# A deformable patch tokenizer rebuilt: convolution by slabs of the contraction, sampling points in squares of 8 rows by 4 columns, places spread by matmuls

## The reference, cut to what matters

```python
off = conv(x, offset_w, stride 16) + offset_b     # 2*256 offsets for each of 5 x 5 patches
py = 16*ho + ki + dy;  px = 16*wo + kj + dx       # 256 points of a patch, each moved by (dy, dx)
y0, x0 = floor(py), floor(px)
sampled = gather(y0, x0)*wy0*wx0 + gather(y0, x0+1)*wy0*wx1 \
        + gather(y0+1, x0)*wy1*wx0 + gather(y0+1, x0+1)*wy1*wx1
out = einsum('bhwkc,ock->bohw', sampled, dconv_w)
yn = batch_norm(out) * gamma + beta;  tokens = gelu(yn)
```

## Time and profile before

| | |
|---|---|
| median of 3 runs | 1245.86 us (1242.81 to 1247.65) |
| span of the profiled execution | 1245.7 us |
| PE busy | 913.0 us, 73% of the span |
| DVE busy | 587.2 us, 47% |
| ACT, POOL busy | 385.2 us, 301.6 us |
| mean granted TensorE clock | 0.829 |

### The profile page before, as it was taken

The page is one execution under the profiler, slowest core; times in us unless marked ns, Lnnn a source line. Parts: engine busy times, 40 slices in busy tenths (PEclk is TensorE's granted clock), DMA queues, the critical chain, the costliest instruction groups (busy, mean ns, idle before and its releaser), DMA issues. The chain is left out here.

```text
span 1245.7 us, 25546 instructions
## 1 busy us (share of the span) xinstructions
PE 913.0 (73%) x10115; PEld 768.6 (62%) x10115; DVE 587.2 (47%) x1245; ACT 385.2 (31%) x675; POOL 301.6 (24%) x291
## 2 busy tenths in 40 slices
PE   4937777769962993589985578487859999286584
PEld 1427777448852993478874566364549999265572
DVE  1639999445434323565442346554461111464463
ACT  0149888022220220244333223243201121143131
POOL 2048888023103231331110010100122322200100
PEclk9969999867875997699887589786777999697695
DMA  3559887570007552000000600000516992100000
GB/s 118 155 153 224 208 209 188 171 204 15 2 14 243 130 124 60 1 2 2 1 2 1 170 3 3 1 3 2 140 38 161 253 241 39 29 3 1 2 4 20
DMA packets 66359, 103.98 MB, mean 83 GB/s; under 512 B 15980, under 2 KB 50128, under 8 KB 66256
## 3 DMA queue, kind: packets, MB, share of 16 engines
q1 hardware_dynamic: 57776, 94.36, 29.5%
q0 software_dynamic: 5120, 4.88, 2.0%
q10 hardware_dynamic: 3360, 3.28, 0.7%
HBM read 92.45 MB, written 10.58 MB: 83 GB/s over the span
## 5 line engine op out<-in xcount | busy, mean ns | idle before, releaser
L1736 PE MATMUL ps_rows<-stage_strip,stage_hat_y 128*128 128x144 f32 x800 | 109.0, 293 | 40.0 <-DVE stage_product L1767 24.2
L1736 PEld LDWEIGHTS ps_rows<-stage_strip,stage_hat_y 128*128 128x128 f32 x800 | 101.6, 192 | 47.3 <-ACT stage_hat_y L1695 21.2
L1767 DVE TENSOR_TENSOR stage_product<-ps_rows,stage_hat_x 128x1296 f32<-128x1296 f32 x80 | 68.5, 898 | 14.1 <-PE ps_rows L1736 14.1
L1718 POOL TENSOR_SCALAR stage_hat_x<-stage_hat_x 128x480 f32<-128x480 f32 x41 | 74.3, 1813 | 3.2 <-ACT stage_hat_x L1693 3.0
L1775 DVE TENSOR_REDUCE stage_samples<-stage_product 128x1440 f32 x40 | 66.2, 1655 | 9.3 <-DVE stage_product L1767 9.3
L2543 DVE TENSOR_TENSOR L_ffnhid<-L_ffnact_gate,L_ffnbank_u 128x300 f32<-128x300 f32 x32 | 14.9, 467 | 117.6 <-ACT L_ffnact_gate L2561 117.6
L1690 ACT ACTIVATE stage_hat_y<-stage_hat_y,stage_w_minus_row 80x1280 f32<-80x1280 f32 x40 | 54.5, 1362 | 29.4 <-DMA stage_hat_y<-places_y 28.8
L1524 PE MATMUL ps_conv<-stage_w_offset_w,stage_patches 128*100 128x512 f32 x96 | 45.5, 628 | 17.2 <-DMA stage_patches<-in_patchesT 17.2
L1708 POOL TENSOR_TENSOR stage_hat_x<-stage_pos_xT,stage_w_window_x 128x240 f32<-128x240 f32 x80 | 48.4, 626 | 18.2 <-DVE stage_product L1767 16.5
L1695 ACT ACTIVATE stage_hat_y<-stage_hat_y 80x1280 f32<-80x1280 f32 x40 | 50.2, 1254 | 0.0
L1097 PE MATMUL L_attnbank_q<-L_attnhT,L_attnwq 128*128 128x200 f32 x192 | 42.7, 369 | 6.9 <-DVE L_attnqT L1262 6.7
(11 more groups left out here) (433 smaller groups left out, 2231.1 us busy)
## 6 DMA issues: line engine op xcount, KB each, us to landing
stage_hat_y<-places_y SPq DMA_DIRECT2D x40, 400.0 KB
stage_strip<-in_strips SPq DMA_DIRECT2D x40, 315.0 KB
L_ffn_win<-in_L_ffn_Win SPq DMA_DIRECT2D x10, 1152.0 KB
stage_L_ffn_win<-in_L_ffn_Win SPq DMA_DIRECT2D x6, 1152.0 KB
L_ffnranks<-stage_ranks SPq DMA_DIRECT2D x16, 400.0 KB
L_ffn_win<-in_L_ffn_Win SPq DMA_DIRECT2D x8, 768.0 KB
L_ffn_wout<-in_L_ffn_Wout SPq DMA_DIRECT2D x10, 576.0 KB
stage_L_ffn_wout<-in_L_ffn_Wout SPq DMA_DIRECT2D x6, 576.0 KB
```

The source lines that it names most:

```text
L1718: nc.gpsimd.tensor_scalar(x, x, 1.0, 1.0, ALU.min, ALU.subtract).then_inc(s["hat_x"], 1)
L1736: mm = nc.tensor.matmul(ps[:, p % 2, bank, at * cols:(at + 1) * cols], hat_y[:, p, g, h * P:(h + 1) * P], rhs.rearrange("q j c x -> q (j c ...
L1767: last = nc.vector.tensor_tensor(split(product[:, p % 2, slots.start * cols:slots.stop * cols]), ps[:, p % 2, banks, 0:used * cols].rearra ...
```

## The change

The order of the points within a patch changes: the 256 points of a patch are cut into 2 halves of 8 rows, each into 4 squares of 8 rows by 4 columns (32 points). A square's window is 12 rows by 8 columns.

- **Loads.** The separate loading block goes. `offset_w` and the patches come slab by slab (6 slabs of 128 of the contraction, first for 400 tokens, then for the other 400), the other constants behind them, in the block of `offsets`.
- **Convolution.** For the y offsets the patches are the weights as before (100 tokens, now 256 columns), for the x offsets the weight matrix is the stationary side (128 points, 400 columns), so that x places come out turned. ScalarE adds the x bias, VectorE the y bias. The turning matmuls, the copy of y places, the origin subtractions and the DRAM tensor `places_y` go.
- **Sampling.** Each step spreads its y places over partitions by 10 matmuls with a 0/1 matrix `spread` of 100 x 64 into PSUM; ScalarE makes `hat_y` from there (640 elements). The rows are mixed by 40 matmuls of 64 x 32 weights over 96 columns, each in one of 8 tiles of the array (2 halves of the rows x 4 squares). VectorE works on 960 elements, and multiplies step i before it sums step i - 1. The 40 steps are written out without loops. The test for far points runs beside the first steps.
- **General path.** The code for far points stands in a block of its own behind the near path, under an `If` that these inputs don't take.

```diff
+GROUP_Y, GROUP_X = PATCH // KHALVES, 4
+COL_GROUPS = PATCH // GROUP_X
+WINDOW_Y, WINDOW_X = GROUP_Y + 2 * MARGIN, GROUP_X + 2 * MARGIN
...
+HALF_P = P // KHALVES
+ROWS_Y = IMG_PER_TILE * WINDOW_Y
...
+                for half in range(2):
+                    cols = slice(half * half_cols, (half + 1) * half_cols)
+                    for c in range(SLABS):
+                        rows = slice(c * P, (c + 1) * P)
+                        if not half:
+                            sp.dma_start(weights[:, c, :], ins["offset_wT"][rows, :]).then_inc(slab_loaded[0][c], 16)
+                        sp.dma_start(patches[:, c, cols], ins["patchesT"][rows, cols]).then_inc(slab_loaded[half][c], 16)
+                    if not half:
+                        for dst, src in consts:
+                            sp.dma_start(dst[:], src).then_inc(consts_loaded, 16)
                 load_rest(sp)
...
+                def convolve_y(t, c):
+                    return nc.tensor.matmul(ps[0:TILE_TOKENS, bank_y(t), 0:KPOINTS], patches[:, c, t * TILE_TOKENS:(t + 1) * TILE_TOKENS], weights[:, c, 0:KPOINTS],
+                                            start=(c == 0), stop=(c == SLABS - 1))
+
+                def convolve_x(half, h, c):
+                    return nc.tensor.matmul(ps[:, bank_x(half, h), 0:half_cols], weights[:, c, KPOINTS + h * P:KPOINTS + (h + 1) * P],
+                                            patches[:, c, half * half_cols:(half + 1) * half_cols], start=(c == 0), stop=(c == SLABS - 1))
...
+                for c in range(SLABS):
+                    pe.wait_ge(slab_loaded[0][c], 32)
+                    for t in range(half_tiles):
+                        mm = convolve_y(t, c)
...
+                    for h in range(KHALVES):
+                        mm = convolve_x(0, h, c)
...
+                for c in range(SLABS):
+                    pe.wait_ge(slab_loaded[1][c], 16)
+                for t in range(half_tiles, TILES):
...
+                        mm = convolve_y(t, c)
+                    mm.then_inc(s["conv_y_in_psum"], 1)
+                for h in range(KHALVES):
+                    pe.wait_ge(s["placed_y"], 3 + h)
+                    for c in range(SLABS):
+                        mm = convolve_x(1, h, c)
+                    mm.then_inc(s["conv_x_in_psum"], 1)
+
...
+                        act.wait_ge(s["conv_x_in_psum"], KHALVES * half + h + 1)
+                        nc.scalar.activation(k.rel_x[:, h, half * half_cols:(half + 1) * half_cols], ps[:, bank_x(half, h), 0:half_cols], ACT.Identity,
+                                             bias=bias_x[:, h:h + 1]).then_inc(s["placed_x"], 1)
...
+                    dve.wait_ge(s["conv_y_in_psum"], t + 1)
+                    nc.vector.tensor_tensor(k.rel_y[:, t, :], ps[0:TILE_TOKENS, bank_y(t), 0:KPOINTS], bias_y[:], ALU.add).then_inc(s["placed_y"], 1)
...
+                    for m, op in enumerate((ALU.min, ALU.max)):
+                        nc.vector.tensor_reduce(k.range_y[0:TILE_TOKENS, m, t:t + 1], k.rel_y[:, t, :], AX_X, op).then_inc(s["reduced"], 1)
...
+                nc.gpsimd.tensor_copy(k.spread[:].rearrange("q n (r j) -> q n r j", j=IMG_PER_TILE), own.unsqueeze(2).to_broadcast(shape)).then_inc(s["spread"], 1)
...
+                    for i, ho, t, p in steps:
+                        if i >= BUFFERS:
+                            sp.wait_ge(s["rows_in_psum"], i - BUFFERS + 1)
+                        for h in range(KHALVES):
+                            sp.dma_start(strip[HALF_P * h:HALF_P * h + ROWS_Y, p], ins["strips"][ho][t][h]).then_inc(strip_loaded[p], 16)
+
...
+                    def spread_places(i, ho, t, p):
+                        if i >= 2:
+                            pe.wait_ge(s["hat_y_abs"], i - 1)
+                        for g in range(GRID):
+                            for h in range(KHALVES):
+                                mm = nc.tensor.matmul(ps_places[HALF_P * h:HALF_P * (h + 1), i % 2, g * P:(g + 1) * P], k.spread[:, ho * GRID + g, :],
+                                                      k.rel_y[:, t, h * P:(h + 1) * P], start=True, stop=True)
+                        mm.then_inc(s["places"], 1)
+
+                    def mix_rows(i, ho, t, p):
+                        pe.wait_ge(s["hat_y"], i + 1)
+                        pe.wait_ge(strip_loaded[p], 32 * (i // BUFFERS + 1))
+                        if i >= 2:
+                            pe.wait_ge(s["multiplied"], i - 1)
+                        for g in range(GRID):
+                            for b in range(COL_GROUPS):
+                                left = PATCH * g + GROUP_X * b
+                                out = slice(QUAD * b, QUAD * (b + 1))
+                                for h in range(KHALVES):
+                                    rows = slice(HALF_P * h, HALF_P * (h + 1))
+                                    mm = nc.tensor.matmul(ps[out, i % 2, h, g * cols:(g + 1) * cols], hat_y[rows, p, g, out],
+                                                          strip[rows, p, :, :, left:left + WINDOW_X].rearrange("q j c x -> q (j c) x"), start=True, stop=True)
+                        mm.then_inc(s["rows_in_psum"], 1)
...
+                    spread_places(*steps[0])
+                    spread_places(*steps[1])
+                    pe.wait_ge(joined, 1)
+                    nc.tensor.matmul(ps_far, any_row[:], any_row[:], start=True, stop=True).then_inc(counted, 1)
+                    for step in steps:
+                        if step[0] == 1:
+                            pe.wait_ge(far_known, 1)
+                        mix_rows(*step)
+                        if step[0] + 2 < STEPS:
+                            spread_places(*steps[step[0] + 2])
...
+                    for i, ho, t, p in steps:
+                        act.wait_ge(s["places"], i + 1)
+                        if i >= BUFFERS:
+                            act.wait_ge(s["rows_in_psum"], i - BUFFERS + 1)
+                        y, x = as_row(hat_y[:, p]), points(hat_x[:, p])
+                        nc.scalar.activation(y, places_in_psum(i % 2), ACT.Abs, bias=w["minus_row"][:]).then_inc(s["hat_y_abs"], 1)
+                        act.wait_ge(s["hat_x_sub"], i + 1)
+                        nc.scalar.activation(x, x, ACT.Abs).then_inc(s["hat_x_abs"], 1)
+                        act.wait_ge(s["hat_y_abs"], i + 1)
+                        nc.scalar.activation(y, y, ACT.Relu, scale=-1.0, bias=1.0).then_inc(s["hat_y"], 1)
...
+                    def finish(i):
+                        pool.wait_ge(s["hat_x_abs"], i + 1)
+                        x = points(hat_x[:, i % BUFFERS])
+                        nc.gpsimd.tensor_scalar(x, x, 1.0, 1.0, ALU.min, ALU.subtract).then_inc(s["hat_x"], 1)
...
+                            own = k.rel_x[:, h, t * TILE_TOKENS:(t + 1) * TILE_TOKENS].rearrange("q (j n) -> q n j", n=TOKENS)[:, ho * GRID:(ho + 1) * GRID, :]
+                            last = nc.gpsimd.tensor_tensor(hat_x[:, p, h * GRID * IMG_PER_TILE:(h + 1) * GRID * IMG_PER_TILE, :].rearrange("q (g j) x -> q g j x", j=IMG_PER_TILE),
+                                                           own.unsqueeze(3).to_broadcast(shape), w["column"][:].unsqueeze(1).unsqueeze(1).to_broadcast(shape), ALU.subtract)
+                        last.then_inc(s["hat_x_sub"], 1)
+                        if i:
+                            finish(i - 1)
...
+                    def multiply(i):
+                        dve.wait_ge(s["hat_x"], i + 1)
+                        dve.wait_ge(s["rows_in_psum"], i + 1)
+                        if i >= 2:
+                            dve.wait_ge(s["summed"], i - 1)
+                        nc.vector.tensor_tensor(products(i % 2), in_psum(i % 2), weights_x(i % BUFFERS), ALU.mult).then_inc(s["multiplied"], 1)
+
+                    def add_up(i):
+                        dve.wait_ge(s["multiplied"], i + 1)
+                        into = k.samples[:, :, :, i * GRID * IMG_PER_TILE:(i + 1) * GRID * IMG_PER_TILE]
+                        nc.vector.tensor_reduce(into.rearrange("q h c w -> q h w c"), products(i % 2), AX_X, ALU.add, negate=True).then_inc(s["summed"], 1)
+
+                    for i, ho, t, p in steps:
+                        multiply(i)
+                        if i:
+                            add_up(i - 1)
+                    add_up(STEPS - 1)
+                    dve.wait_ge(s["summed"], STEPS)
+
...
+            def far_steps(eng, step, before=None):
+
+                far = eng.value_load(k.far[0:1, 0:1], min_val=0, max_val=1)
+                with eng.If(far == 1):
...
-            with nc.Block() as block:
-                @block.sync
-                def _(sp):
-                    for dst, src in load:
-                        sp.dma_start(dst, src).then_inc(arrived, 16)
-                    sp.wait_ge(arrived, 16 * len(load))
 
             def load_rest(sp):
 
+                for dst, src in load:
```

(16 more changed lines are left out.)

527 lines of the change are left out of this document (246 added, 281 removed).

## The result

The changed kernel takes 1200.27 us (median of 5 runs, 1193.13 to 1200.58) where the kernel before takes 1245.86 in the same job: ratio 0.9631, 95% interval 0.9596 to 0.9667, so 3.7% faster. The forecast was 1179 with a range of 1160 to 1222: the range held it, but only two thirds of the gain came (46 us of 67). The profiled execution is the fastest of the five: 1193.13 us, span 1191.0.

A forecast was written before the change was run, and what follows sets the result against it. Sampling was taken as bound by VectorE at about 3.5 us a step, after the change by TensorE at 2.6. From 1245.7, minus 30.6 (start), minus 40.4 (steps), plus 4 (general path) gave 1179 us, range 1160 to 1222.

The forecast's parts named there:

- The band with a chance of 0.60: Main forecast for the whole kernel: a sampling step of 2.4 to 2.9 us, total 1171 to 1191 us.
- parts or supply: Sampling step at 3.2 to 3.3 us, from TensorE's parts sharing more or instructions arriving too slowly; chance 0.20.
- Part 1: Loads and convolution: first row mix at about 54.3 us instead of 84.88, 30.6 us gained.
- the slow start: Start of the convolution: TensorE begins at the lower clock, which costs 3.0 us.
- Part 2: Sampling steps: 2.6 us each against 3.5, TensorE longest; 104.8 us instead of 145.2, 40.4 us gained.
- Instruction supply: Sampling: 200 TensorE instructions a step at a ceiling of 63 per us, 3.2 us a step, 1202; shared chance 0.20.
- the shared parts: Rival in the mix: TensorE's array parts share more, step 3.2 to 3.3 us, total 1202 to 1206; shared chance 0.20.
- Its other side: Instruction supply under strip load in sampling: 40 per us, step 5.0 us, kernel 1273; clock or starved supply together 0.07.
- Part 3: Behind the last reduce: reading the flag, jumping over the general path and a barrier, 4 us lost.

The follow-up runs named there:

- after_again: The changed kernel once more with no edit, on the chip of the runs beside it: median 1198.6 us, ratio 0.962 to the kernel before.
- m2_loop: Changed kernel with TensorE's sampling in a loop of two steps, places and spread copied to fixed buffers, two strip buffers: 1186.5 us, ratio 0.951 to the kernel before.

## Why the prediction was right, and where it was off

The direction and the range were right. The mechanism given for the step was not: the forecast had TensorE's own work as the pace and nothing for the supply of its instructions. The band with a chance of 0.60 (1171 to 1191) was missed by the median, and what came was the branch "parts or supply", which had 0.20 and for whose sake the range reached to 1222.

The sum was 1178.7 for the span; the profiled span is 1191.0, so 12.3 us are to be explained, term by term.

- *Part 1* was right in mechanism and 3.0 us too careful: first mix at 51.29, forecast 54.3. The first slab came at 5.20 where I had put 7, and the convolution ended at 44.97, forecast 47.8; the slow start was there (3.73 us for the first eight records, 1.89 later: half the pace, though the granted clock is given as 1.00 in that stretch, as no record of it begins before 10.7 us).
- *Part 2, the terms of one step.* Mix with its change of form 1.13 (forecast 1.06 + 0.13), spread with its 1.24 (1.20 + 0.13), VectorE 2.30 (2.26; its pace is 2.35 with the wait for its own sum), ScalarE 0.79 + 0.46 + 0.73 = 1.98 (2.0), GpSimd 1.28 + 2 x 0.49 = 2.26 (2.24). An undisturbed step was 2.37 where the terms made 2.5. That the eight parts run side by side was right. The Trainium skill (TensorE: Matmul & The Clock Gate, "Wait — 56ns, not 53.3ns?") has matmuls start at least 25 ns apart; here 80 records start within 1.13 us, 14 ns apart, so in parts of the array that floor does not hold.
- *Part 2, the step that failed*: "I add 0.1 for waits: 2.6 us a step". The term for supply was at nothing, on the ground that nothing in the trace showed starvation. It was 0.75 us a step: the 36 steps from the fourth mix to the last took 110.8 us (65.81 to 176.6, where the last 80 records of a merged row begin), 3.08 each, 17.2 more than forecast; the three before them 14.5 instead of 7.8, 6.7 more, of which 2.8 are one stall and most of the rest the granted clock of 0.50 around it, where the prediction had 1.00 in the steps; the tail 5.95 instead of 3.4, since VectorE had two steps left to sum. Together 26.5: of the 40.4 us, 13.9 were gained. The rival "Instruction supply" had mechanism and size (63 per us, 3.2 us a step, 1202), and stood with the shared parts at 0.20 together. Its other side, 40 per us beside the strips, did not come: the strips cost 0.26 us a step.
- *Part 3*: 6.2 us between sum and projection, forecast 4.3; 1.9 more.
- *Behind the tokenizer*, where I had put the same time as before: 1002.3 us from the projection on, 1015.3 before. I take these 13.1 us for the spread of that stretch, which is as large for one and the same code (last section); but the three profiled executions of the changed kernel lie at 991.3 to 999.2 us there (from the statistics on) and the one of the kernel before at 1008.8, so it is not shown that none of it is the change's.

-3.0 + 26.5 + 1.9 - 13.1 = 12.3. Against the median (1200.3) the forecast was some 21.5 low: these 12.3, 7.1 by which the profiled execution ran faster than the median, and 2.1 of its time outside its span. That the span came within 12 us is partly luck; without the 13.1 us behind the tokenizer it would have been 1204. The tokenizer alone gained 41.6 us (230.37 to 188.74) of the 67 forecast, and the medians 45.6.

"Against it: nothing in the trace shows such starvation" was true of the window of the earlier trace rows, and no evidence: the kernel before had nowhere asked for 200 instructions in 2.5 us for long (no 10 us of it hold more than 72 records per us). In that window TensorE waited for other engines more than for "issue":

```profile
PE L_ffnbank_h L658 <- DVE L_ffnv_heads L806: 1.1, 1, 1.1
PE L_ffnbank_o L698 <- ACT L_ffnpT L915: 0.6, 1, 0.6
PE L_ffnbank_b L616 <- issue: 0.2, 1, 0.2
```

So its 63 per us was not a limit that could be read there, and that it came so near the measured 62 to 68 is partly luck.

The Trainium skill (Runtime: NRT & Kernel Launch, "Instruction fetch mechanics") describes code coming in blocks of 256 instructions, the crossing of a block "mostly hidden", and control flow as a reason to unroll. The block agrees (254 or 256 records from wait to wait here); hidden it is not, once 256 instructions run in less than the 3.6 to 4.0 us that a block takes, and here the loop is the cheaper form (2.42 us a step against 3.1). It also gives TensorE room for 2048 instructions, by which the body of some 800 would stay; the run agrees, and a larger body was not tried.

## What to carry to other kernels

Count the instructions of an engine per us before unrolling: on TensorE written-out code came at 62 to 68 records per us over stretches of 20 us beside the strips, and at 68 to 74 without them. A stage of small matmuls that could run faster than that reaches its own pace only in a loop whose body stays, or with fewer and longer matmuls. When the stage runs into "issue" waits at even distances, look at the packets of the code queue in that window, and tell supply from columns by changing the one without the other. Keep bursts of loads away from the first steps of a new block that is written out.

## What the runs showed of the hardware that I had not expected

- A block of code (16 KB, some 256 instructions) came every 4.0 us beside the strips and every 3.6 without; shorter matmuls did not hasten it (20 packets in 80 us with 96 and with 48 columns). TensorE went on 2.4 to 3.0 us after a packet's start in the changed kernel, although the packets themselves took 1.0 to 1.6 us.
- A TensorE loop of some 800 instructions fetched in its first turn and ran the other 7 without a packet, with 88 records per us.
- Jumping over the general path's unused code cost all engines 4.8 us together with its barrier, reading a flag 0.9.
- The same code behind the tokenizer took from 991.3 us (after_again, clock 0.836) to 1019.6 (m2_loop, clock 0.822), counted from the statistics to the end of the span; in the kernel before 1008.8 at 0.829. With the clock at 0.834 to 0.838 it was 991.3 to 1004.9, at 0.822 to 0.827 it was 1009.3 to 1019.6. The mean granted clock goes with it; what moves the clock from one execution to the next stayed open, and so does whether it is the whole cause. With such a spread, edits worth 5 us in the tokenizer do not show in a total.
